# Expert tiles of a mixture-of-experts kernel: the gathered rows are transposed by a DMA instead of by TensorE, and ScalarE issues the weight and bias loads

## The reference

```python
x = x + xattn(layernorm(x), ctx)                  # attention, first stage of the kernel
h = layernorm(x).reshape(4096, 1024)
logits = h @ gate_w.T + gate_b
topk_logits, topk_idx = top_k(logits, 4)          # 4 of 32 experts for each row
topk_weight = softmax(topk_logits)
# for every (row, chosen expert e):
gate = minimum(h @ w_gate[e] + b_gate[e], 7)
up   = clip(h @ w_up[e] + b_up[e], -7, 7)
act  = (up + 1) * gate * sigmoid(1.702 * gate)
out  = act @ w_down[e] + b_down[e]
y    = sum over the 4 experts of out * topk_weight
x = x + y
```

## Time and profile before

| | |
|---|---|
| median of three runs | 3279.18 us (3278.2 to 3282.7) |
| the profiled execution, its own time | 3284.01 us |
| its span in the trace | 3282.2 us |
| TensorE busy in the span | 3120.8 us (95%) |
| VectorE, ScalarE, POOL busy | 1720.9, 1280.6, 595.1 us |
| mean granted TensorE clock | 0.973 of full speed |

### The profile page before, as it was taken

The page is one execution under the profiler, slowest core; times in us unless marked ns, Lnnn a source line. Parts: engine busy times, 40 slices in busy tenths (PEclk is TensorE's granted clock), DMA queues, the critical chain, the costliest instruction groups (busy, mean ns, idle before and its releaser), DMA issues.

```text
span 3282.2 us, 46620 instructions
## 1 busy us (share of the span) xinstructions
PE 3120.8 (95%) x15456; PEld 1609.9 (49%) x15457; DVE 1720.9 (52%) x2851; ACT 1280.6 (39%) x1299; POOL 595.1 (18%) x502
## 2 busy tenths in 40 slices
PE   6799899995999999999999999999999999999997
PEld 3455555553455444455455444544555445455553
DVE  4576767774453544554544545444455444454432
ACT  3553434422342434443433434344344333343421
POOL 0023323322111111111111111111111111111111
PEclk8899999997999999999999999999999999999999
DMA  4123222354564555556555655655565655555432
GB/s 149 64 104 124 103 84 104 104 166 146 144 171 117 148 154 154 174 159 198 155 155 150 173 154 166 192 173 144 142 171 164 197 156 153 154 163 144 110 63 58
DMA packets 210439, 468.03 MB, mean 143 GB/s; under 512 B 57761, under 2 KB 57761, under 8 KB 210114
## 3 DMA queue, kind: packets, MB, share of 16 engines
q1 hardware_dynamic: 164514, 314.84, 27.2%
q0 software_dynamic: 45856, 152.33, 22.2%
HBM read 354.64 MB, written 112.46 MB: 142 GB/s over the span
## 4 chain that ended last, share of the span: by engine, by line
PE 71%; DMA 3%; SPq 1%; issue 1%; ACT 0%; DVE 0%; POOL 0%; ACTq 0%; POOLq 0%; DVEq 0%
PE psG L1167 22%; PE psU L1167 22%; PE psY L1189 22%; PE psX L1173 4%; PE psA L1180 2%; DMA bias<-in_L_ffn_b_down 2%; DMA idxg<-slots 0%; SPq L959 0%; DMA idxs<-slots 0%; SPq L112 0%; DMA acc<-y,idxs 0%; SPq L962 0%; DMA xg<-xn_tab,idxg 0%; ACT aT L1057 0%; DVE gt L1122 0%
## 5 line engine op out<-in xcount | busy, mean ns | idle before, releaser
L1189 PE MATMUL psY<-W,aT 128*128 128x512 f16 x3456 | 777.9, 382 | 23.1 <-ACT aT L1057 23.1
L1167 PE MATMUL psG<-W,xT 128*128 128x512 f16 x3456 | 772.4, 380 | 2.9 <-ACT xT L1053 2.9
L1167 PE MATMUL psU<-W,xT 128*128 128x512 f16 x3456 | 769.4, 379 | 0.0
L1167 PEld LDWEIGHTS psG<-W,xT 128*128 128x128 f16 x3456 | 338.8, 98 | 413.0 <-issue 6.1
L1189 PEld LDWEIGHTS psY<-W,aT 128*128 128x128 f16 x3456 | 339.7, 98 | 406.2 <-ACT aT L1057 24.5
L1167 PEld LDWEIGHTS psU<-W,xT 128*128 128x128 f16 x3456 | 338.2, 98 | 375.6
L1114 DVE SCALAR_TENSOR_TENSOR y<-bias,idxs,y 128x1024 f32<-128x1024 f32 x144 | 185.0, 1284 | 544.7 <-ACT y L1064 544.7
L123 DVE SCALAR_TENSOR_TENSOR W<-stage,W 128x2048 f16<-128x2048 f32 x192 | 438.7, 2285 | 4.8 <-ACT W L118 4.8
L1021 POOL DMA_INDIRECT acc<-y,idxs x144 | 227.4, 1579 | 1011.9 <-DVE y L1114 996.3
L1064 ACT ACTIVATE y<-psY,idxs 128x1024 f32<-128x1024 f32 x144 | 160.5, 1114 | 604.6 <-DMA idxs<-slots 577.9
L118 ACT ACTIVATE W<-stage 128x2048 f16<-128x2048 f32 x192 | 365.1, 1902 | 10.8 <-issue 5.5
(11 more groups left out here) (136 smaller groups left out, 2305.1 us busy)
## 6 DMA issues: line engine op xcount, KB each, us to landing
stage<-in_L_ffn_w_gate SPq DMA_DIRECT2D x64, 1024.0 KB
stage<-in_L_ffn_w_up SPq DMA_DIRECT2D x64, 1024.0 KB
stage<-in_L_ffn_w_down SPq DMA_DIRECT2D x64, 1024.0 KB
stage<-in_x SPq DMA_DIRECT2D x32, 512.0 KB
xr<-in_x SPq DMA_DIRECT2D x32, 512.0 KB
acc<-xr SPq DMA_DIRECT2D x32, 512.0 KB
xn_tab<-x2h SPq DMA_DIRECT2D x32, 512.0 KB
bias<-in_L_ffn_b_down SPq DMA_DIRECT2D x32, 512.0 KB, 13.6
```

Of the source, the lines that this page charges most:

```text
L1167: op = pe.matmul(ps[:], xT[:, k, :, a], weights(par, c, offset + k * I, I), start=k == 0 and n == 0, stop=k == KH - 1 and n == 2)
L1189: op = pe.matmul(psY[:, h * HALF:(h + 1) * HALF], aT[:, k, :, a], weights(par, c, 2 * KH * I + k * H + h * HALF, HALF), start=k == 0 and n ...
```

## The change

The gathered rows are no longer transposed by TensorE. SP issues a transposing DMA from `xg` to a new tile `xT_next` (128 x 16 x 128 fp16, 512 KB), once tile i's rows are gathered and ScalarE has copied the tile before out of `xT_next`. ScalarE copies `xT_next` to `xT` (`take_rows`, in the place of `evac_x`), when the `up` matmuls no longer read `xT`. POOL's next gather waits for the transposing DMA instead of for TensorE. Since a 2-byte transposition can't keep an HI and an LO together in one word, the rows hold first all HI, then all LO; `x2h` and `xn_tab` are laid out so. `psX` goes. SP issues neither weight chunks nor bias rows any more: ScalarE does, at the end of its step, and `LOAD` spreads the chunks two by two.

```diff
-        x2h = sb("x2h", [P, 2, H, 2], F16)
+        x2h = sb("x2h", [P, 2, 2, H], F16)
...
-    LOAD = [[3, 4], [5], [6, 7, 8]]
+    LOAD = [[3, 4], [5, 6], [7, 8]]
...
-        xT = sb("xT", [P, KH, P, 2], F16)
+        xT = sb("xT", [P, 2 * KH, P], F16)
+        xT_next = sb("xT_next", [P, 2 * KH, P], F16)
...
         @block.sync
         def _(sp):
+            def transpose_rows(i):
+
+                sp.dma_start_transpose(out=xT_next[:, :, :], in_=xg[:, :]).then_inc(s_xtr, 16)
+
             load_slots(sp, idxg, 0, s_idxg)
-            load_bias(sp, 0, 0)
             sp.wait_ge(s_xg, 16)
             load_slots(sp, idxg, 1, s_idxg)
-
-            def step(i, e, j, more, prev_guard):
-
-                sp.wait_ge(s_xg, 16 * i + 32)
+            transpose_rows(0)
+
+            def step(i, prev_guard):
+
+                alone(sp, s_xg, 16 * i + 32, s_past)
                 load_slots(sp, idxg, i + 2, s_idxg)
+                alone(sp, s_xTev, i + 1, s_past)
+                transpose_rows(i + 1)
...
             with pool.Fori(1, last) as j:
-                pool.wait_ge(s_X, j + 3)
+                pool.wait_ge(s_xtr, 16 * j + 48)
                 gather(j + 3)
...
-            def evac_x(i):
-                act.wait_ge(s_X, i + 1)
-                act.activation(xT[:].rearrange("p k q a -> p (k q a)").bitcast(F32), psX[:], ACT.Copy).then_inc(s_xTev, 1)
+            def take_rows(i):
+                act.wait_ge(s_xtr, 16 * i + 16)
+                act.activation(xT[:].rearrange("p k q -> p (k q)").bitcast(F32),
+                               xT_next[:].rearrange("p k q -> p (k q)").bitcast(F32), ACT.Copy).then_inc(s_xTev, 1)
...
+                def loads():
+                    if j == MIN_TILES - 1:
+                        alone(act, s_y, t0 + 1, s_past)
+                        load_bias(act, e + 1, 1 - par)
+                    for c in LOAD[j]:
+                        def load(c=c):
+                            alone(act, s_wlo, NCHUNK * e + NCHUNK + c - RING + 1, s_past)
+                            load_chunk(act, e + 1, c)
...
-                evac_x(i + 1)
+                alone(act, s_U, i + 1, s_past)
+                take_rows(i + 1)
                 act.wait_ge(s_act, i + 1)
                 act.activation(ahl[:, :, HI], av[:], ACT.Copy, scale=S_ACT).then_inc(s_ahi, 1)
                 guarded(act, prev_guard, lambda: weigh_y(i - 1))
+                if j is not None:
+                    guarded(act, more, loads)
...
                 rows_times(psU, par, KH * I, s_U)
-                pe.wait_ge(s_xg, 16 * i + 32)
-                transpose_rows()
                 guarded(pe, prev_guard, lambda: down(i - 1, 1 - par if first else par))
```

More of the change, by code:

```diff
@@ L533, in step @@
                     act.wait_ge(s_xs2, tile(bt, n + 1))
-                    act.activation(x2h[:, n % 2, :, HI], xs2[:], ACT.Copy, scale=S_ROWS).then_inc(s_hi2, 1)
+                    act.activation(x2h[:, n % 2, HI, :], xs2[:], ACT.Copy, scale=S_ROWS).then_inc(s_hi2, 1)
                 if b1 is not None:
@@ L980, in step @@
                 guarded(sp, prev_guard, prev)
[L981 to L986, removed]
             with sp.Fori(0, PAIRS) as pair:
@@ L991, in _ @@
                     t0, t1 = start_of(sp, e), start_of(sp, e + 1)
-                    some = pair < PAIRS - 1
-                    more = [None if par == 0 else some] * 2 + [some]
                     for j in range(MIN_TILES):
-                        step(t0 + j, e, j, more, pair > 0 if par == 0 and j == 0 else None)
-                    if par == 0:
-                        sp.wait_ge(s_y, t0 + 1)
-                        load_bias(sp, e + 1, 1 - par)
-                    else:
-                        with sp.If(some):
-                            sp.wait_ge(s_y, t0 + 1)
-                            load_bias(sp, e + 1, 1 - par)
+                        step(t0 + j, pair > 0 if par == 0 and j == 0 else None)
                     with sp.If(t1 > t0 + MIN_TILES):
                         with sp.Fori(t0 + MIN_TILES, t1) as i:
-                            step(i, e, None, None, None)
+                            step(i, None)
             tt = start_of(sp, E)
@@ L1028, in _ @@
             gather(0)
-            pool.wait_ge(s_X, 1)
-            gather(1)
-            pool.wait_ge(s_X, 2)
-            gather(2)
-            pool.wait_ge(s_X, 3)
-            gather(3)
+            for i in range(1, 4):
+                pool.wait_ge(s_xtr, 16 * i)
+                gather(i)
             scatter(0)
             with pool.Fori(1, last) as j:
-                pool.wait_ge(s_X, j + 3)
+                pool.wait_ge(s_xtr, 16 * j + 48)
                 gather(j + 3)
@@ L1066, in _, with step @@
             act.sem_inc(s_y0, 1)
-            evac_x(0)
-            def step(i, e, par, t0, j, more, prev_guard):
+            load_bias(act, 0, 0)
+            take_rows(0)
+            def step(i, e, par, t0, j, more, later, prev_guard):
+                def loads():
[6 more added lines that the diff above has]
+                            load_chunk(act, e + 1, c)
+                        if c < NCHUNK or par == 1:
+                            load()
+                        else:
+                            guarded(act, later, load)
                 def free_gate_up():
@@ L1099, in _ @@
                     for j in range(MIN_TILES):
[L1100 removed]
+                        step(t0 + j, e, par, t0, j, pair < PAIRS - 1 if par else None, pair < PAIRS - 1,
                              pair > 0 if par == 0 and j == 0 else None)
@@ L1166, in rows_times @@
                     for n, (a, c) in enumerate(PASSES):
-                        op = pe.matmul(ps[:], xT[:, k, :, a], weights(par, c, offset + k * I, I),
+                        op = pe.matmul(ps[:], xT[:, a * KH + k, :], weights(par, c, offset + k * I, I),
                                        start=k == 0 and n == 0, stop=k == KH - 1 and n == 2)
                 op.then_inc(done, 1)
-            def transpose_rows():
-                for n in range(KH):
-                    op = pe.transpose(psX[:, n * P:(n + 1) * P], xg_w[:, n * P:(n + 1) * P], ident[:])
-                op.then_inc(s_X, 1)
             def transpose_act(i):
```

23 lines of the change are left out of this document (9 added, 14 removed).

## The result

The changed kernel is slower: 3335.4 us median of four runs (3327.9 to 3344.2), beside 3280.9 us for the kernel before on the same chip. The ratio is 1.0159, with an interval of 1.0145 to 1.0174. I had predicted 3136.

A forecast was written before the change was run, and what follows sets the result against it. TensorE, busy 95%, was taken to bound the kernel. 3284.0 - 125.3 + 4 - 22 = 3140.7 us; the profiled execution stood 4.8 us above the median, so about 3136 us was forecast, range 3112 to 3225.

The forecast's parts named there:

- step 2: SBUF-to-SBUF transposition of 512 KB: taken as 5 us from issue to landing, hidden behind TensorE's 15.98 us step.
- X: Time of the transposing DMA from issue to landing, taken as 5 us from transfers of the same size.
- The loop through `xg`: Transposition, gather, index load through a single buffer: X + 6.6 us, fitting the 15.98 us step up to X = 9.4.
- The slack at the copy: ScalarE's copy of `xT_next`: needs the transposition at 26.8 us after the step's start, may be as late as 30.9.
- The slow transposition: Rival: the transposing DMA sets the step, from X = 10.3 on; about 4,415 us with 16-byte pieces; chance 0.14.
- the partial loss: Rival: late transpositions, gathers or chunks lose up to two thirds of the gain, 3160 to 3225 us; chance 0.10.
- 1, `psX` off TensorE, -125.3: TensorE's transposed rows: 144 sets at 0.87 us no longer run there, -125.3 us.
- step 6: `x2h` written without interleaving by ScalarE and VectorE, 32 tiles: taken as 0, with an end of -13 us.
- 4, the start, +4: Before the first gate matmuls: index load issue, transposition and copy make the start 4 us later.
- 3, ScalarE's issues cost nothing: ScalarE's copy and its chunk and bias issues: at most 3 us of issues on an engine busy 39%, costing nothing.
- 5, bias rows, -22: Bias rows issued ahead of the chunks land earlier for `evac_a`: 22 of about 28 us back, ends 0 and 28.

The follow-up runs named there:

- the two kernels with one queue: Against the kernel before, SP issues two chunks a step and bias rows once an expert: 3123.6 us with the transposing DMA ahead of them, 3252.8 us without it.
- ScalarE's loads alone: The kernel before, with weight chunks and bias rows issued by ScalarE as in the change and no transposing DMA: 3250.3 us.
- loads on SP: The changed kernel with weight chunks and bias rows issued by SP again, at their old places behind the load of `idxs`: 3237.8 us.
- the one with 512-byte pieces: The changed kernel with ScalarE's weight chunks in the expert loop loaded in 512-byte pieces instead of 2 and 4 KB: 3405.0 us.
- the swap of two issues: The changed kernel with SP issuing the transposition ahead of the next index load instead of behind it: 3154.6 us.

## Why the prediction was wrong

**The step that failed** is step 2, "The transposing DMA": "I take X = 5", used as one constant, and "it may land at 11 to 14 rather than 11; the transposition then starts up to 2 us late, which the slack to 26.8 covers". As a price of the DMA by itself 5 was good; alone it takes 4.3 to 4.4 us. But the delay changed what it met. The gather beside scatter and chunks landed at about 15.4, the transposition went out at 15.8 in place of 12.1, and there ScalarE's burst begins. X then has two ranges, by the count less 0.9: up to 8.2 us when it is ahead of the burst by 1 us or more (13.5 when by less), and 10 to 28.7 when it is behind. Slack covers a delay of a fixed duration, not a duration that the delay itself multiplies by four.

The loop through `xg` was mis-sized too. I had X + 6.6 us, with 5.2 from the gather's start to the next index load. In the two steps shown above that part took 9.5 us (1534.62 to 1544.12) and 6.1 (1555.27 to 1561.39). With 9.5 the loop fits a step of 15.98 only up to X = 5.1, an estimate from these rows, and not up to 9.4. So there was hardly any slack where I saw some 4 us.

**The price of it.** 175 us of idle TensorE and 36 us of lower clock are 211; less the some 10 us by which the first stage ended earlier (below), that is about the 199 between the forecast's 3136 and 3335. The slack at the copy was sized rightly: issued at 15.8, with the copy due by 30.9, a transposition may take some 15 us, which is 16 by the count, and 14 of the 145 are over that. The other eight of the 22 stops are in steps next to one of these, by way of the loop.

**The rivals.** The slow transposition had the mechanism in part, TensorE waiting for `xT` behind the DMA, but I had its cause in the size of the pieces, so that it would hold in every step. The pieces are of 256 bytes, and 2.7 us of data (last section) is within the 1 to 3 us that I gave for that size. I had even written down the right ingredients under the partial loss, "gather, scatter, chunks and the transposition meet in one step", and bounded it at 3225 since I had no row in which two queues meet. The bound from the earlier trace rows was there: bias rows behind 3 MB took 13.62 us. With that as an upper end for X the loop is 20.2 us, and the range would have crossed the time before.

By "The three transpose paths" in "VectorE: DVE Perf Modes" of the Trainium skill, my estimate was 20.9 us for this tile. This case's trace does not bear that estimate out: the first transposition of the changed kernel, 16 squares of 128, lands after 4.43 us. The 261 GB/s of "Latency and other measured facts" in "DMA: Bandwidth & Descriptors" of the Trainium skill is above what one window here shows, about 197 GB/s (last section).

**Steps that held.** *1, `psX` off TensorE, -125.3*: between the two kernels with one queue, with and without the transposing DMA, there are 130 us. That is -125.3, with the start's +4 and some -11 of step 6. *4, the start, +4*: rows land at 785.6 and the gate starts at 792.9, 7.3 us where before it was 3.8: +3.5. *3, ScalarE's issues cost nothing*: held; TensorE's waits for `aT`, where late chunks would show, are 6.8 us in all. *5, bias rows, -22*: -23.1 in the balance above, and 33 us with ScalarE's loads alone, slightly beyond my end of 28.

**Mis-sized**: step 6, `x2h`, taken as 0. ScalarE's write takes 1056 ns in place of 1354, VectorE's 1224 in place of 1383, 14.6 us over both engines for 32 tiles. Here are the groups after:

```profile
L786 DVE SCALAR_TENSOR_TENSOR x2h<-xs,x2h 128x1024 f16<-128x1024 f32 x32 | 39.2, 1224 | 15.1 <-ACT x2h L534 15.1
...
L534 ACT ACTIVATE x2h<-xs 128x1024 f16<-128x1024 f32 x32 | 33.8, 1056 | 43.1 <-DVE xs L737 43.1
```

The first index load of the expert stage is issued at 776.9 in place of 787.7 in these two profiles. Other kernels with the same first stage issue their first transposition between 781.5 and 789.7, so not all of the 10.8 us can be laid to `x2h`; it was not tried alone.

**What stays open**: why the transposition behind 3 MB of another queue takes 20 to 28 us, while bias rows behind 3 MB of the same queue took 13.6 and loads on SP held it to 16.6. Turns between the queues packet by packet would fit, but no run shows them: the one with 512-byte pieces was meant to and did not. The scatter that runs beside most of the late ones was not tested alone either.

## What to carry to other kernels

Price a new DMA at the moment at which it will be issued, beside what its neighbours issue within a microsecond or two, and take the slowest transfer of the trace that stood behind a burst as its upper end, not the median of its size. A DMA of many small packets that something waits for belongs ahead of the bulk loads: in one queue with them behind it, or, in another queue, 2.8 us ahead, which was enough here when 1 us was not always. And when a delay is "covered by slack", look up what runs at the place to which it moves.

## What the runs showed of the hardware that I had not expected

**A transposing DMA is quick and cheap in bytes, not in packets.** Packets, MB and share of 16 engines of SP's queue in the changed kernel, first with the transposition nearly alone (1452 to 1457 us; it is issued at 1452.37), then behind the burst (1420 to 1447 us, ScalarE's queue first):

```profile
q1 hardware_dynamic: 2224, 0.53, 57.8%
```

```profile
q10 hardware_dynamic: 1488, 3.15, 58.1%
q1 hardware_dynamic: 2224, 0.53, 21.4%
```

0.578 x 16 x 5 us over 2224 packets is 20.8 ns each (2048 of them are the transposition's, of 256 bytes); behind the burst it is 0.214 x 16 x 27 / 2224 = 41.6 ns. The total went from 210,439 packets to 512,040, and the small ones cost the kernel with one queue no wait of TensorE's. Sixteen engines at 20.8 ns for 2048 packets are 2.7 us of data, about 197 GB/s.

**An issue can be held.** SP's issue of a transposition takes 1.7 us at least and 2.0 in the median (an index load 0.34), and up to 11.6 behind a burst, with all of SP's program behind it. With the swap of two issues the longest is 5.2. These are the groups of the changed kernel and of that one (shortest, median and longest ns):

```profile
L968 SPq DMA_TRANSPOSE xT_next<-xg x145: 1721/2008/11598, 786.7 to 3296.6; - x145
```

```profile
L968 SPq DMA_TRANSPOSE xT_next<-xg x145: 1507/1811/5224, 785.7 to 3088.5; - x145
```

**Other transfers pay too.** The gather's median from issue to landing went from 4.4 us to 6.2 in the changed kernel.
